# A transformer kernel on one core: stacks loaded chunk by chunk, and another order of steps and streams in the two attention phases

## What is computed

```python
x = x + layernorm(attention0(layernorm(x)))   # low-rank q and kv, norm on both, rotary on half a head
x = x + layernorm(ffn0(layernorm(x)))         # silu gate, int8 weights with scales
x = x + layernorm(attention1(layernorm(x)))   # plain qkv
x = x + layernorm(ffn1(layernorm(x)))
# both attentions: 16 heads of 16 channels, causal over 2048 tokens
scores = einsum('bhqd,bhkd->bhqk', q, k) / 4
y = einsum('bhqk,bhkd->bhqd', softmax(where(causal, scores, -inf)), v)
```

## Time and profile before

| | us |
|---|---|
| median of three runs | 1305.29 (1305.1 to 1305.45) |
| the profiled execution | 1312.36 |
| its span, first to last instruction | 1310.6 |
| first attention phase, first S to last YT | 90.8 to 523.5 |
| second attention phase | 728.6 to 1161.9 |

### The profile page before, as it was taken

One profiled execution on the slowest core, in us unless ns is written; L12 is line 12 of the kernel. 1 busy time (PEld: TensorE's weight loads), 2 busy tenths in 40 slices (PEclk: granted clock), 3 DMA queues, 4 the chain that ended last, 5 costly groups with the idle time before them and its releaser, 6 DMA issues.

```text
span 1310.6 us, 35514 instructions
## 1 busy us (share of the span) xinstructions
PE 1183.3 (90%) x14872; PEld 557.0 (42%) x14872; DVE 1040.9 (79%) x2746; ACT 721.0 (55%) x919; POOL 334.9 (26%) x561
## 2 busy tenths in 40 slices
PE   5767999999999998799979789999999999987996
PEld 4432333433433433556645233333344333354664
DVE  6857898999999961778863778899899999438776
ACT  2442455777777787234342434477776777853332
POOL 2322101123310122334432211111322111314443
PEclk9976898999999999899999678899999999998999
DMA  5353000200200000000025310002002000000000
GB/s 168 117 151 107 15 2 3 82 20 4 80 21 2 3 3 2 1 33 1 1 74 186 94 60 2 2 18 84 4 20 83 3 3 2 3 1 1 10 24 33
DMA packets 31600, 49.95 MB, mean 38 GB/s; under 512 B 7245, under 2 KB 24143, under 8 KB 31431
## 3 DMA queue, kind: packets, MB, share of 16 engines
q1 hardware_dynamic: 25376, 41.95, 10.6%
q0 software_dynamic: 5488, 5.34, 1.4%
q10 hardware_dynamic: 576, 0.39, 0.1%
HBM read 32.56 MB, written 14.68 MB: 36 GB/s over the span
## 4 chain that ended last, share of the span: by engine, by line
PE 64%; DVE 19%; DMA 6%; issue 3%; POOL 3%; ACT 3%; SPq 1%; ACTq 0%; POOLq 0%; DVEq 0%
PE ps L940 62%; DVE m_tile L833 6%; DVE ps L835 3%; DMA k_parts<-parts 3%; DMA q_stack<-m_rows 2%; POOL q_stack L508 2%; DVE region_p L693 1%; DVE stats L680 1%; PE ps L1087 1%; ACT region_p L622 1%; DMA q_parts<-parts 1%; DVE region_p L891 1%; PE ps L935 1%; SPq L396 1%; SPq L401 1%
## 5 line engine op out<-in xcount | busy, mean ns | idle before, releaser
L622 ACT ACTIVATE region_p<-ps 128x1024 f32<-128x1024 f32 (+3 forms) x640 | 542.0, 895 | 284.2 <-PE ps L940 280.8
L833 DVE TENSOR_REDUCE m_tile<-ps 128x1 f32<-128x512 f32 x768 | 499.2, 684 | 50.6 <-PE ps L940 48.4
L940 PE MATMUL ps<-k_stack,q_stack 96*32 96x512 bf16 (+3 forms) x5120 | 412.1, 372 | 23.8 <-DVE v_all L741 7.6
L940 PE MATMUL ps<-q_stack,k_stack 99*32 99x512 bf16 (+3 forms) x5120 | 344.2, 360 | 14.6 <-DMA q_stack<-m_rows 10.8
L940 PE MATMUL ps<-region_p,v_all 128*17 128x512 f32 (+3 forms) x2560 | 291.0, 532 | 4.5 <-POOL region_p L513 4.5
L940 PEld LDWEIGHTS ps<-k_stack,q_stack 96*32 96x32 bf16 x5120 | 136.2, 97 | 336.3 <-DVE m_tile L833 152.5
L835 DVE CUSTOM_DVE_ANT_0 ps<-ps,causal 128x128 f32<-128x128 f32 (+3 forms) x512 | 248.1, 497 | 31.8 <-PE ps L940 30.1
L940 PEld LDWEIGHTS ps<-q_stack,k_stack 99*32 99x32 bf16 x5120 | 126.4, 98 | 134.2 <-ACT region_p L622 39.6
L513 POOL TENSOR_SCALAR_AFFINE_SELECT region_p<-region_p 128x512 f32<-128x512 f32 x128 | 81.1, 635 | 286.3 <-ACT region_p L622 284.0
L940 PE MATMUL ps<-region_a,w_ffn 128*128 128x512 f16 x512 | 124.1, 388 | 6.1 <-DVE region_a L725 5.2
L656 ACT ACTIVATE k_stack<-ps,cols 128x512 f32<-128x512 f32 x64 | 44.0, 687 | 128.2 <-PE ps L940 125.8
(11 more groups left out here) (93 smaller groups left out, 907.8 us busy)
## 6 DMA issues: line engine op xcount, KB each, us to landing
k_parts<-parts SPq DMA_DIRECT2D x16, 384.0 KB, 8.3
q_parts<-parts SPq DMA_DIRECT2D x16, 384.0 KB, 8.6
q_stack<-q_parts SPq DMA_DIRECT2D x32, 192.0 KB
k_stack<-k_parts SPq DMA_DIRECT2D x32, 192.0 KB
q_stack<-q_parts SPq DMA_DIRECT2D x32, 128.0 KB
k_stack<-k_parts SPq DMA_DIRECT2D x32, 128.0 KB
X<-in_x SPq DMA_DIRECT2D x4, 512.0 KB, 6.3
q_stack<-q_parts SPq DMA_DIRECT2D x32, 64.0 KB
```

Source lines behind the costliest of these rows:

```text
L622: nc.scalar.activation(probs[:, o.j % SLOTS, 2 * o.hp:2 * o.hp + 2, o.off:CH], psT[:, o.k % 2, :, o.off:CH], ACT.Exp, scale=SCALE).then_in ...
L833: nc.vector.tensor_reduce(maximum, scores, AX.X, ALU.max).then_inc(s.ring_free, 1)
L940: return pe.matmul(o, a, b, start=first, stop=last)
```

## The change

The greedy model goes. The order of the 16 steps and the merge of the three streams are written out: `STEP_ORDER` as a list, and `TURNS`, a string of 1152 letters, one for each turn. The number of turns of each kind, the work of each and the prices are as before. The order of the items within each stream is as before within a step.

SyncE's loads of groups 2 and 3 are split: the q part of chunk Q of group g + 2 is loaded when the last T of step (g, Q) has been issued, the k part of chunk c when the last T of the last step that reads this chunk has. In the new step order the k parts of group 2 all follow step 3, with the q part of chunk 3; for group 3 one q part and one k part follow each of steps 4, 5, 6 and 7.

```diff
-STEP_ORDER = [(g, Q) for g in range(NG) for Q in (range(NCH) if g % 2 == 0 else reversed(range(NCH)))]
-LEAD, LEAD_REST = 280, 4
+STEP_ORDER = [(0, 0), (0, 1), (0, 2), (0, 3), (1, 3), (1, 2), (1, 1), (1, 0),
+              (2, 2), (2, 3), (3, 3), (3, 2), (2, 1), (3, 1), (2, 0), (3, 0)]
+TURNS = (
+    "SSSSSSSSSSSSSSSSSSSSSMSSSSSSSSSSSTSTSSTSSTSSTSTSVTSTSSSVSSVVSSSSSSSSSSSSSSSSSSSSSSSSSSSSSSSSSSSS"
+    "SSSSSSSSSSSSSMSSSSSSSSSSSTSTSSTSSTSTVSTSSTVTSTSSTSVSTSSTVSVMSTSSTYSTSVSSTSTSSSTSVSSTTSSVSTTSSVSS"
+    "TTSVSTSVSTSSTVSSTSSTSVSSTSTSVSSTSTSVSSTSVSSTSSTSVSTMSTSSSSVSSTSTSSVSTSSTSVSTSTSYTSVSSTTSVSTSTVST"
...
+    "STVVMSTSSTSVTSTSSVTSTVTYTVTSTSSVSTSTYSTVTSSTSTMSVSTSVSTSSTSTVTSTVTSTVTTVMTVTTVVVYTTYTTTTVTTVVVY"
+)
...
+    for turn in TURNS:
+        if turn == "S":
             n, h, r, c = s_units[si]
...
-    LAST_T = {o.g: o.k for o in ORDER if o.kind == "T"}
+    LAST_T = {o.n: o.k for o in ORDER if o.kind == "T"}
+    LAST_KEY_STEP = {(g, c): n for n, (g, Q) in enumerate(STEPS) for c in range(Q + 1)}
...
+                def load_stacks(g, c):
+                    load_queries(g, c)
+                    load_keys(g, c)
...
-                for g in range(2, NG):
-                    sp.wait_ge(s.t_filled, L * T_N + LAST_T[g - 2] + 1)
-                    for c in range(NCH):
-                        load_stacks(g, c)
+                for n, (g, Q) in enumerate(STEPS):
+                    if g + 2 < NG:
+                        sp.wait_ge(s.t_filled, L * T_N + LAST_T[n] + 1)
+                        for c in range(NCH):
+                            if c == Q:
+                                load_queries(g + 2, c)
+                            if n == LAST_KEY_STEP[g, c]:
+                                load_keys(g + 2, c)
```

More of the change, by code:

```diff
@@ L96, in plan_attention @@
     kts = [list(range(TPC * Q, TPC * Q + TPC)) + list(range(TPC * Q)) for _, Q in steps]
[L97 to L101, removed]
-    order = []
-    pe = dve = act = pool = 0.0
@@ L104, in plan_attention @@
[L104 to L134, removed]
-            n, h, r, c = s_units[si]
[L136 to L140, removed]
@@ L141, in plan_attention @@
+    t_list = [(n, i, kt, hp) for n in range(len(steps)) for i, kt in enumerate(kts[n]) for hp in range(2)]
+    pv_list = [(n, i, kt) for n in range(len(steps)) for i, kt in enumerate(kts[n])]
+    order = []
+    ring = si = mt = yt = ti = pi = sel = 0
+    for turn in TURNS:
+        if turn == "S":
+            n, h, r, c = s_units[si]
             si += 1
-            s_done += width // P
             last = si == len(s_units) or s_units[si][0] != n
-            order.append(Step("S", n, g, Q, h=h, r=r, c=c, last=last, ring=ring))
@@ L145, in plan_attention @@
[L145 to L150, removed]
-            g, Q = steps[mt]
-            pe += 70
-            dve = max(dve, pe + PE_LAT) + 150
-            ring_free[ring % RING] = dve + SEM_NS
-            order.append(Step("MT", mt, g, Q, ring=ring))
-            ring += 1
-            m_rows[mt] = dve + 2800
-            mt += 1
-        elif kind == "YT":
-            g, Q = steps[yt]
-            pe += 300
-            dve = max(dve, pe + PE_LAT) + 500
-            ring_free[ring % RING] = dve + SEM_NS
-            order.append(Step("YT", yt, g, Q, ring=ring))
-            ring += 1
+            order.append(Step("S", n, *steps[n], h=h, r=r, c=c, last=last, ring=ring))
+        elif turn == "M":
+            order.append(Step("MT", mt, *steps[mt], ring=ring))
+            mt += 1
+        elif turn == "Y":
+            order.append(Step("YT", yt, *steps[yt], ring=ring))
@@ L166, in plan_attention @@
             yt += 1
[L167 to L169 removed]
+        else:
+            n, i, kt, *hp = t_list[ti] if turn == "T" else pv_list[pi]
+            Q = steps[n][1]
             diag = kt >= TPC * Q
             off = P * (kt - TPC * Q) if diag else 0
[L172 to L201 removed]
@@ new lines, in plan_attention @@
+            last = i == len(kts[n]) - 1
+            if turn == "T":
+                order.append(Step("T", n, *steps[n], kt=kt, off=off, hp=hp[0], k=ti, j=ti // 2, first=diag,
+                                  last=last and hp[0] == 1))
+                ti += 1
+            else:
+                sel += diag
+                order.append(Step("PV", n, *steps[n], kt=kt, off=off, first=i == 0, last=last, j=pi,
+                                  sel=sel if diag else None))
+                pi += 1
@@ L202, in plan_attention @@
+        ring += turn in "SMY"
+    assert (si, ti, pi) == (len(s_units), len(t_list), len(pv_list)) and mt == yt == len(steps)
     return steps, order
@@ L387, in _, with load_queries @@
             for L in range(2):
-                def load_stacks(g, c):
+                def load_queries(g, c):
                     h0 = g % 2 * HG
@@ L398, in load_stacks, with load_keys @@
                                      ).then_inc(stack_in[g % 2][c], 16)
+                def load_keys(g, c):
+                    h0 = g % 2 * HG
+                    for first, n in STACK_RUNS:
+                        rows_ = slice(first * DH, (first + n) * DH)
                         src = (D["k_parts0"][c, 0:n, :, g * HG:(g + 1) * HG, :] if L == 0 else
```

43 lines of the change are left out of this document (9 added, 34 removed).

## The result

The changed kernel takes 1276.01 us (median of 4 runs, 1274.14 to 1278.07) against 1305.37 (1305.1 to 1306.41, with a fourth run beside the three of the table before): ratio 0.9774, 95% interval 0.9757 to 0.9791. The forecast was 1293 with a range from 1276 to 1306: the right direction, less than half of the size (29 us measured, 12 forecast), and the time lies on the very edge of the range, which is luck.

What follows compares the result with a forecast made beforehand. It took TensorE to bound the middle and VectorE the head. Head 60.9, middle 350.2 and tail 17.3 gave 428.4 us against 432.4; with 2 for finer merging, 6 a layer, 12 in all: 1293 us, range 1276 to 1306.

Steps and rivals of the forecast that it cites:

- the 64 us of waits: First attention phase: of 432.4 us TensorE works 368 and is held up for 64; only these can change.
- the signs that the prediction gave: What the new profile should show: phase lengths, clock, TensorE's idle, tail length, and no waits on transfers at named steps.
- (1) Head: Up to the first T of step 1: VectorE's 55.6 us plus 1.2, a restart of 3.1 and 1.0, 60.9 us.
- (2) Middle: First T of step 1 to last S: TensorE's 332 us, restart 4.3, waits 13.9 at the old 4.2%, 350.2 us.
- part 4: Finer merge in the middle: fewer runs of three S; pieces sum to 6 us less, 2 a layer taken.
- (3) Tail: After the last S: TensorE's 11.9 us of work plus waits of the last T, 17.3 us together.
- Rival B: The merge does more, in middle, restart at step 1 and tail: 8 to 15 us a layer, 1275 to 1289; chance 0.20.
- Rival A: Three ring banks set the middle's waits and no order mends them: 1295 to 1301, chance 0.20.
- (5) Chunk loads: Loads of groups 2 and 3: only their times move, hidden behind TensorE's work; nothing in the sum.
- The collision named for step 5: Step 4's six transfers run against step 5's maxima: up to 1.8 us a layer, none taken, kept in the range.
- The restarts: First T of steps 0 to 3: 3 to 4.5 us each; two fewer gain 7 to 8 us a layer.
- From the sum to the time: Profiled 1312.4 us less 12.2 is 0.9907 of it; applied to the median 1305.3 it gives 1293 us.

Runs made afterwards that it cites:

- e9: Kernel before, with two spare matmuls of 384 columns behind each S of the S-only stretches to keep TensorE busy; 1312.31 us, ratio 1.0032.
- e5: Old turns up to the first T of step 4, then the changed kernel's turns, with three S more and one V fewer; new loads; 1296.91 us, ratio 0.9914.
- e6: Changed kernel with turns 367 to 854 re-merged so that S come three in a row; 1303.97 us, ratio 0.9975.
- e2: Kernel before with only the new chunk loads, old step order and old merge; 1305.71 us, ratio 0.9993.
- e1: Changed kernel with groups 2 and 3 loaded whole, as before; 1308.69 us, ratio 1.0005.
- e7: Kernel before, its steps and loads kept, with newly searched turns; 1268.22 us, ratio 0.9707.
- e11: Kernel before, its steps and loads kept, with turns from a longer search than in e7; 1257.62 us, ratio 0.9636.
- e10: Kernel before, with group 1's loads held back eight T, to the first T of step 1; 1305.44 us, ratio 0.9994.
- e12: Changed kernel's chunk loads, with turns and step order, (1,3) before (0,3), searched as long as for e11; 1268.75 us, ratio 0.9717.
- e8: Changed kernel's steps and loads, with turns searched in the same way as e7; 1269.95 us, ratio 0.9707.

## Why the prediction was right in direction and wrong in size

**What bounds, and what can't change.** Right. Work and instructions are the same, TensorE bounds the middle, VectorE the head, and only the 64 us of waits moved. Of the signs that the prediction gave, one came true: the phases are not 424 to 429 us long but 418.3 and 416.5. The others did not: no T of step 5 and no S of step 10 waits for a transfer, and VectorE doesn't idle in the long stretch of S. The clock is full from 61 us on, up to the tail, and not from 71, and TensorE lost 10 us between the first T of step 1 and the last S, not 12 to 18.

**(1) Head: 60.9 forecast, 57.7 and 57.2 measured.** VectorE's 55.6 us of work took only 1.6 to 2.1 more; the 5.3 that I added (1.2, a restart of 3.1, 1.0 for the long stretch) were 3.2 to 3.7 too many. In the long stretch the mean clock is 0.62 (32 of its 42.3 us are at the lower level) and VectorE works through it, 41.21 of 42.30 us. So it cost at most the 1.1 us by which it is longer than VectorE's busy time, since VectorE set the pace. The Trainium skill ("TensorE: Matmul & The Clock Gate", section "HAM oscillation — how this bites in real kernels") asks for TensorE's work without idle gaps. This trace agrees where T resume, as e9 shows (2.2 to 2.5 us), and not within this stretch. The wait on the maxima did go, as said.

**(2) Middle: 350.2 forecast (348.2 with the 2 us of part 4), 342.1 measured.** All that was lost in the piece of step 1 was 2.5 and 1.8 us, where I had 4.3 for its restart. The rest of the waits was 7.7 us on 316.6 of work, 2.4%, where I had carried over the old order's 4.2%, 13.9 us. That is the step that failed most: a rate of waits read in the old order was taken for a property of the kernel, and the order is what sets it.

**(3) Tail: 17.3 forecast, 18.5 and 17.3 measured.** Right within 1.2; the last YT still waits 0.81 us for the copy, as in the earlier trace rows.

The sum: 57.7 + 342.1 + 18.5 = 418.3, against 428.4 - 2 = 426.4. Head 3.2, restart 1.8, waits 4.2 (13.9 less the 2 of part 4 less 7.7), less 1.2 of the tail: 8.0 of the missing 8.1 us of the first phase.

**(4) The finer merge.** The right mechanism, named and then priced at a third: my own count of pieces gave 6 us and I took 2. e5 puts it at 4 to 6 us a layer behind the first T of step 4 alone. e6 shows how much hangs on the spacing of S, for threes in 487 of 1152 turns cost 13 us a layer; it doesn't show what the new merge gives over the old one. Rival B, "the merge does more" (1275 to 1289), with a chance of 0.20, is what happened. Two of its parts came true, half of the middle's waits and half of the restart at step 1; the tail gave nothing, and the head gave 3 us that it didn't name. Rival A took the bank waits for a matter of three banks that no order mends. The runs say otherwise: 88.2 us of such waits became 33.3 with the same three banks. The Trainium skill ("Perfetto Trace Analysis", section "Optimization Strategy") says that gaps which keep coming back can mean too few buffers, which pointed the same way as rival A. Whether a fourth bank would help as well was not run.

**(5) Chunk loads.** My sum had nothing for them, and alone they bring nothing (e2); no S of steps 8 or 10 waits. The stall that they prevent was understated: 15 us a layer in e1, for I read the 18.8 us of issues as the length of the load, and it takes 32 from the first issue to the first use of the last chunk. The collision named for step 5 did not come: no T waits there. With the changed string the new step order needs them (e1); the gain doesn't need the new step order (e7, e11).

**The restarts.** The prediction explained 3 to 4.5 us each by the lower clock and by waits that follow. e9 bears out about 2.2 of them as clock, and the two layers of e7 1.8; the rest was booked to it without proof. It also shows why the cure isn't spare work: there the spare matmuls lengthened the stretch of S by about as much as the restart gained. In both layers of e11, and in the first of e7, the same steps in the same order go from step 1 to step 3 with no restart, at a clock of 1.00; there the T of one step go on until the maxima of the next have come. Not settled by these runs is what the other 1 to 2.5 us of a restart are, and where the rest goes of what e10 gives back.

**From the sum to the time.** Scaling by the profiled run's ratio was sound: phases 30.6 us shorter, medians 29.4. Starting at 1312.4, 7 us above the median, did little harm since only differences were used; that the two agree within 1.3 us is partly luck, for the two profiled spans differ by 37.1.

## What to carry to other kernels

When an order of work is replaced, don't carry over the old order's rate of waits: cut both orders at the same landmarks, price what each engine has to do between them, and take the larger one as the floor; here good merges came within 0 to 1 us of that floor in most pieces. Test which part of a change is the lever by doing each alone: here loads and step order gave nothing with the old planner, and a better merge by itself, with the old steps and loads, gave more (1257.6 us) than the change with all three (1276.0). Size a transfer by when its last consumer can start (32 us here), not by how long its issues take (19 us).

## What the runs showed of the hardware

- 24 transfers between DRAM and the stacks (64 to 192 KB each) were issued in 18.9 us, and the first S that needed the last of them started 32 us after the first issue (e1); in the first layers of e1 and e12 alike the first user of the last chunk started 13 us after the last issue had ended.
- Three such transfers on SyncE's queue went with 5.60 us for the small DMAs of the maxima, issued by GpSimd, instead of 1.64 (e8); beside the loads of the kernel before it was 5.13.
- A restart at the lower clock cost 2.2 to 2.5 us (e9: two T 1.15 us apart, 0.60 at the upper level) and 1.8 us between the two layers of e7; spare matmuls kept the clock up and cost 1.9 us in the stretch they filled (e9).
- A stretch of 42.3 us with a mean clock of 0.62 was bounded by VectorE, busy for 41.2 of it, so the clock cost at most 1.1 us there (changed kernel).
